# Looks at the weights moved later in the opening, and the first tile of the second deep layer ended a step later, with all-row products of the first keys

## The chip, the cores and the metric

The kernel runs on one core of a Trainium2 chip. Its engines work side by side, each on its own queue of instructions in order, and meet through semaphores: TensorE (PE in the profile, its weight loads PEld), VectorE (DVE), ScalarE (ACT), GpSimd (POOL) and SyncE (SP), which here only issues DMAs. The metric is the device time of one launch in microseconds (us), the median over runs.

## The reference

A transformer layer, fp32, on 8 sequences of 512 rows and 256 features:

```python
x = x + attention(layernorm(x))   # qkv = xn @ qkv_w.T, 16 heads of 16, rotary q and k,
                                  # mask = (same block of 64 | i < 4 | j < 4 | |i - j| <= 128) & (j <= i)
                                  # softmax(q k / 4) @ v, then @ out_w.T
n = layernorm(x)
h = silu((n @ w1.T) * s1) * ((n @ w2.T) * s2)      # 256 -> 1024, weights -1, 0, 1
h = gelu((h @ h1.T) * s1h)                         # 1024 -> 1024, erf form
h = gelu((h @ h2.T) * s2h)                         # 1024 -> 1024
x = x + (h @ w3.T) * s3                            # 1024 -> 256
```

Each query sees at most its own and the previous 128 keys, and the first four keys (the global keys).

## The kernel before, in words

Sequences are worked in rounds. Round r computes the feed-forward layers of sequence r, beside it the attention of sequence a = r + 1, and beside that the normalization, the projections and the rotation (rotary embedding) of sequence b = r + 2. The opening is "round -1": attention of sequence 0 and projections of sequence 1, with no feed-forward. Each engine has a function `beside_attention(r)`, a loop over 20 steps n (16 units of attention, a unit being 4 heads of a tile of 128 queries, and 4 steps of tail). Its body is an order written out by hand; the order of the calls in it is the order on that engine. Rounds 0 to 7 begin with `gated(r)` (w1 and w2), and steps 0 to 15 hold the 16 tiles of the two deep layers on TensorE (tiles 0 to 7 the first, 8 to 15 the second), each in four quarters of two k-chunks (`deep_quarter`), spread between the attention's parts of the step. Bank n % 2 takes tile n. Round 7 has no attention beside it.

Unit n of attention: `scores` (PE, step n), `masked_min` (VectorE: mask, minimum; it frees the bank through `s_free`), `exponentials` (ScalarE), `turn_cur` and `turn_prev` (PE transposes, step n + 2), kept by VectorE (`keep_cur`) and ScalarE (`keep_prev`, n + 2), and `weighted_values` (PE). In the opening the scores of two units come together at even steps, VectorE masks both there, and `values` come at even steps. A tile's last unit adds the products of the four first keys, `Vg` x `PgT` (64 rows: 16 heads x 4 keys), and transposes of `rinv_wide`, then `out_projection` i, VectorE's `residual` i, the second layernorm and its transposes.

All small products share one PSUM bank, MISC (bank 6). `misc_free` reads the order of its users from the lists ROUND and OPENING and waits for the one before to have been read: "o0" is output projection 0, "qk0" to "qk3" the projections of q and k (features 0 and 1), "t" the transposes of the normalized input (kept by ScalarE's `keep_xnT`), "gs", "pg", "vg" the first keys' scores, weights and values, "n" the transposes of the second layernorm.

A hidden tile h is kept as two parts, hi (rounded for the fast product) and lo (the rest). ScalarE makes the full value and hi with `gelu` in parts of 4, 2, 1, 1 tiles, POOL the lo (`deep_lo`), and `deep_split` counts them; tile 8's quarter 3 needs tiles 6 and 7 of layer 0.

The fast product is exact only if the weights have no low bits. ScalarE looks at all weights in 11 looks (`check_weights`, one pass over 128 x 2048 words each, counted in `low_summed`), two before the opening and nine at the steps LOOK_STEPS. At step KNOWN - 1 VectorE takes their maximum (`low_bits`), TensorE turns it into one number, VectorE into a flag (`no_low_bits`), and before step KNOWN TensorE reads it and branches to one of two copies of the rest of its program.

SP's queue in the opening: the loads of inputs; then, after look 3 (`low_summed` 4), the staging of the second layer's weights for the looks; then eight copies of weight chunks from DRAM to DRAM (`w_scratch`, `save_weights`); then `save_split`, which writes the split q and k of sequence 1 to DRAM in four parts, then their loads. ScalarE's `split_hi` 2 and 3 (features 1) write the same SBUF tile that saves 0 and 1 read, so they wait for these saves to have landed:

```python
wait(act, split_saved[1 - f][kind], 16 * SAVES * (b - 1 + f))
```

## Time and profile before

| | |
|---|---|
| time before | 1090.91 us, median of 3 runs (1089.97 to 1091.35) |
| the profiled execution | 1091.03 us, span 1089.2 us |
| mean granted TensorE clock | 0.992 of full speed |
| busy: TensorE, its weight loads, VectorE, ScalarE, POOL | 97%, 81%, 59%, 66%, 41% |
| first gated product | 101.7 us |

The profiled execution's time holds the span, from the first to the last instruction, and some 2 us around it. A profile row of a timeline gives start and length in us, the engine and line, operation and operands, and in brackets how long the engine had stood idle before and what ended that. "issue" means that nothing the profile shows was waited for.

### The profile page before, as it was taken

The numbers are of one execution on the slowest core, as the hardware profiler recorded it, in microseconds if no ns is written. First come the engines' busy times: TensorE is split into PE (matmuls) and PEld (weight loads), VectorE is DVE, ScalarE is ACT, GpSimd is POOL, SyncE is SP. The second block draws the span as 40 slices with busy tenths as digits, with TensorE's granted clock in tenths as the row PEclk, the third lists the DMA queues.
The fourth block names the chain that finished last, engine by engine and source line by source line (L and its number), as shares of the span: only waits on it lengthen the run. The fifth ranks groups of instructions, "written<-read, shape, count | busy, mean of one in ns | idle before, by whom it ended". The sixth has DMA issues, their size and how long they took to land.

```text
span 1089.2 us, 21612 instructions
## 1 busy us (share of the span) xinstructions
PE 1056.3 (97%) x7602; PEld 878.5 (81%) x7602; DVE 643.6 (59%) x1988; ACT 718.4 (66%) x1776; POOL 450.1 (41%) x620
## 2 busy tenths in 40 slices
PE   6788999999999999999999999999999999999998
PEld 3457878898788977889778897889878898789887
DVE  5775576556765567655665566755576555555322
ACT  3895676955958658567586566685676955966422
POOL 5552462433624418235263254442362431532433
PEclk9889999999999999999999999999999999999999
DMA  8887469455655357555483654736556355432540
GB/s 317 306 266 244 162 208 301 131 173 175 197 174 155 125 183 232 144 153 183 134 255 104 194 163 145 241 91 198 170 165 194 108 174 185 115 108 76 178 135 21
DMA packets 112797, 190.16 MB, mean 175 GB/s; under 512 B 7216, under 2 KB 66864, under 8 KB 111664
## 3 DMA queue, kind: packets, MB, share of 16 engines
q1 hardware_dynamic: 112256, 182.45, 53.8%
q10 hardware_dynamic: 432, 6.29, 1.4%
q8 instruction: 64, 1.05, 0.4%
q14 instruction: 45, 0.37, 0.1%
HBM read 150.97 MB, written 45.09 MB: 180 GB/s over the span
## 4 chain that ended last, share of the span: by engine, by line
PE 78%; ACT 10%; DVE 7%; issue 3%; POOL 2%; DMA 1%; SPq 0%; ACTq 0%; DVEq 0%; POOLq 0%
PE bank L787 36%; PE bank L757 11%; PE bank L560 5%; PE bank L691 5%; PE bank L814 4%; PE bank L627 4%; PE bank L657 4%; ACT Sm L963 4%; DVE Sm L1162 3%; PE bank L665 3%; PE bank L591 2%; ACT L983 2%; POOL b_lo L1452 2%; PE bank L716 1%; PE bank L704 1%
## 5 line engine op out<-in xcount | busy, mean ns | idle before, releaser
L963 ACT ACTIVATE Sm<-Sm,smin 128x260 f32<-128x260 f32 (+2 forms) x512 | 241.4, 473 | 163.0 <-DVE smin L1162 162.6
L787 PE MATMUL bank<-b_hi,W 128*128 128x512 f32 x512 | 211.0, 412 | 3.9 <-POOL b_lo L1452 3.9
L787 PE MATMUL bank<-a_hi,W 128*128 128x512 f32 x512 | 206.5, 403 | 0.1
L787 PE MATMUL bank<-b_lo,W 128*128 128x512 f32 x512 | 201.1, 393 | 0.0
L787 PE MATMUL bank<-a_lo,W 128*128 128x512 f32 x512 | 200.8, 392 | 0.0
L757 PE MATMUL bank<-x_hi,W 128*128 128x256 f32 x512 | 125.0, 286 | 0.0
L757 PE MATMUL bank<-x_lo,W 128*128 128x256 f32 x512 | 123.4, 283 | 0.0
L1461 POOL TENSOR_TENSOR a_lo<-a_act,a_hi 128x256 fp32r<-128x256 f32 x128 | 94.4, 741 | 61.7 <-ACT a_hi L1014 61.7
L787 PEld LDWEIGHTS bank<-b_hi,W 128*128 128x128 f32 x512 | 96.4, 188 | 24.8 <-POOL b_lo L1452 10.2
L1162 DVE CUSTOM_DVE_ANT_0 Sm<-bank,msk,gmin 128x256 f32<-128x256 f32 x256 | 108.2, 478 | 10.4 <-PE bank L627 7.0
L1213 DVE TENSOR_SCALAR a_sum<-bank,scales 128x512 f32<-128x512 f32 x64 | 48.0, 750 | 105.7 <-PE bank L787 104.9
L787 PEld LDWEIGHTS bank<-a_hi,W 128*128 128x128 f32 x512 | 96.4, 188 | 17.5 <-DVE a_act L1245 0.3
L787 PEld LDWEIGHTS bank<-a_lo,W 128*128 128x128 f32 x512 | 96.5, 188 | 17.1
L787 PEld LDWEIGHTS bank<-b_lo,W 128*128 128x128 f32 x512 | 96.7, 189 | 14.6
L1452 POOL TENSOR_TENSOR a_lo<-a_act,a_hi 128x512 fp32r<-128x512 f32 x56 | 70.9, 1292 | 83.9 <-ACT a_hi L984 83.9
L757 PEld LDWEIGHTS bank<-x_hi,W 128*128 128x128 f32 x512 | 98.1, 192 | 2.7 <-issue 2.7
L1452 POOL TENSOR_TENSOR b_lo<-b_act,b_hi 128x512 fp32r<-128x512 f32 x64 | 80.9, 1292 | 45.2 <-ACT b_hi L984 45.2
L757 PEld LDWEIGHTS bank<-x_lo,W 128*128 128x128 f32 x512 | 98.1, 192 | 0.0
L1245 DVE SCALAR_TENSOR_TENSOR a_act<-bank,scales,silu 128x256 f32<-128x256 f32 x128 | 61.8, 483 | 58.2 <-ACT silu L1020 57.9
L963 ACT ACTIVATION_READ_ACCUMULATOR Sm<-Sm,smin 128x1 f32 x512 | 96.1, 188 | 0.0
L1213 DVE TENSOR_SCALAR b_sum<-bank,scales 128x512 f32<-128x512 f32 x64 | 47.9, 749 | 76.9 <-PE bank L787 75.9
L1177 DVE COPY PT<-bank 128x512 f32<-128x512 f32 x72 | 49.5, 687 | 70.4 <-PE bank L657 67.7
(134 smaller groups left out, 2199.1 us busy)
## 6 DMA issues: line engine op xcount, KB each, us to landing
W<-w_scratch SPq DMA_DIRECT2D x168, 512.0 KB, 4.1
qk_scratch<-split SPq DMA_DIRECT2D x56, 512.0 KB, 4.0
Qs<-qk_scratch SPq DMA_DIRECT2D x112, 128.0 KB, 4.3
Ks<-qk_scratch SPq DMA_DIRECT2D x14, 1024.0 KB, 8.7
w_scratch<-in_ffn_w SPq DMA_DIRECT2D x22, 512.0 KB, 7.1
x_in<-in_x SPq DMA_DIRECT2D x8, 512.0 KB, 7.5
stage_a<-in_ffn_w ACTq DMA_DIRECT2D x2, 2048.0 KB, 9.6
x<-in_x SPq DMA_DIRECT2D x8, 512.0 KB, 3.9
```

The lines of the kernel that those rows point to most:

```text
L560: mm = nc.tensor.matmul(qk_bank(b, n)[:, :], qkv_w[:, kk, col:col + P], xnT[:, kk, :], start=(kk == 0), stop=(kk == NF - 1))
L627: mm = nc.tensor.matmul(bank[2 + half][:, c2 * KEYS + lo:(c2 + 1) * KEYS], Qs[:, pair, half, :], Ks[:, pair, i * P + lo - P:(i + 1) * P], ...
L691: mm = nc.tensor.matmul(out[32 * c:32 * c + 32, :], v[:, i - 1 + side, col:col + 32], turned(a, n)[:, side, c, :], start=(g == 0 and side ...
L757: mm = nc.tensor.matmul(bank[DOWN_BANKS[s % 4]][:, u * HALF:(u + 1) * HALF], lhsT.bitcast(F32) if general else lhsT, rhs, start=(kk == 0 a ...
L787: mm = nc.tensor.matmul(bank[n % 2][:, :], lhsT.bitcast(F32) if general else lhsT, rhs, start=(kk == 0 and part == 0), stop=(kk == NH - 1 ...
L963: ex = nc.scalar.activation(row, row, ACT.Exp, bias=smin[:, r, c:c + 1], scale=-1.0, accum_out=rowsum[:, i % 2, col:col + 1])
L1162: tt = nc.vector.tensor_tensor_reduce(out=unit_scores(n, lo)[:, c, :], in0=ps[:, c2 * KEYS + lo:(c2 + 1) * KEYS], in1=msk[:, int(i == 1), ...
L1177: nc.vector.tensor_copy(turned(a, n)[:, 1, :, :].rearrange("p c q -> p (c q)"), bank[5][:, :])\
L1213: nc.vector.tensor_scalar((b_sum, a_sum)[layer][:, m, :], bank[n % 2][:, :], scales[:, 2 + layer, m:m + 1], None, ALU.mult).then_inc(sum_k ...
L1245: nc.vector.scalar_tensor_tensor(a_act[:, m, half * HALF:(half + 1) * HALF], bank[DOWN_BANKS[s % 4]][:, HALF:SEQ], scales[:, 1, m:m + 1], ...
L1452: nc.gpsimd.tensor_tensor(lo[:, m, :], full[:, m, :], hi[:, m, :].bitcast(F32), ALU.subtract)\
L1461: nc.gpsimd.tensor_tensor(a_lo[:, m, cols], a_act[:, m, cols], a_hi[:, m, cols].bitcast(F32), ALU.subtract).then_inc(up_split, 1)
```

## The change

Four things change.

1. The looks: LOOK_STEPS becomes (1, 3, 5, 7, 9, 11, 13, 15, 16) from (1, 2, 3, 5, 7, 9, 10, 11, 13), and KNOWN becomes UNITS + 3 = 19 from 16, so the flag is found at step 18 and TensorE branches before step 19. The flag's product goes to bank 2, since the values of sequence 1 are by then in banks 0 and 1.
2. In the opening output projection 0 moves from step 7 to step 10 on TensorE (behind "qk3" in MISC's order), its residual on VectorE and the layernorm scalars on POOL from step 8 to 11. ScalarE's `keep_xnT` comes a step earlier for both halves, the second one behind the exponentials.
3. In every round quarter 3 of tile NH (tile 8) is issued in step NH + 1, behind quarter 0 of tile 9, instead of at the end of step NH.
4. `Vg` and `PgT` get 128 rows, the upper 64 cleared by POOL at the start (`g_zeroed`); the products of the first keys contract over all of them.

```diff
-SHIFT, KNOWN = 3, UNITS
-LOOK_STEPS = (1, 2, 3, 5, 7, 9, 10, 11, 13)
+SHIFT, KNOWN = 3, UNITS + 3
+LOOK_STEPS = (1, 3, 5, 7, 9, 11, 13, 15, 16)
...
-OPENING = ("t0", "t1", "qk0", "qk1", "o0", "qk2", "qk3", "o1", "gs", "pg0", "o2", "n0", "pg1", "n1", "n2", "o3",
+OPENING = ("t0", "t1", "qk0", "qk1", "qk2", "qk3", "o0", "o1", "gs", "pg0", "o2", "n0", "pg1", "n1", "n2", "o3",
...
-        Vg = sb("Vg", [HEADS * NGLOB, EMB])
+        Vg = sb("Vg", [P, EMB])
-        PgT = sb("PgT", [HEADS * NGLOB, P])
+        PgT = sb("PgT", [P, P])
...
                         if t == 0:
-                            pe.wait_ge(low_ready, 1)
+                            pe.wait_ge(s_free, HALVES)
...
                         pe.wait_ge(glob_kept, 2 * a + i - 1)
+                        if a == 0 and i == 2:
+                            pe.wait_ge(g_zeroed, 2)
...
                 if with_f and n < DEEP:
                     deep_quarter(r, n, 0, general)
+                if with_f and n == NH + 1:
+
+                    deep_quarter(r, NH, 3, general)
...
-                if with_f and n < DEEP:
+                if with_f and n < DEEP and n != NH:
                     deep_quarter(r, n, 3, general)
...
-                    if (i := tile_at(n, 7)) is not None:
+                    if r < 0 and n == 10:
+                        out_projection(r, 0)
+                    if (i := tile_at(n, 7)) is not None and (r >= 0 or i):
                         out_projection(r, i)
...
-                    pe.wait_ge(s_free, 2 * (KNOWN - 1))
-                    nc.tensor.matmul(bank[0][0:1, 0:1], low_all[:, :], minus_half, start=True, stop=True)\
+                    pe.wait_ge(s_free, HALVES)
+                    nc.tensor.matmul(bank[2][0:1, 0:1], low_all[:, :], minus_half, start=True, stop=True)\
                         .then_inc(low_added, 1)
                 step(-1, n, False)
+                if n >= UNITS:
+                    v_projection(-1, [n - UNITS])
...
-                    if with_q and nq - 1 in LN1_STEPS:
+                    if r >= 0 and with_q and nq - 1 in LN1_STEPS:
                         keep_xnT(r, nq - 1 - LN1_STEPS[0])
+                    if r == -1 and nq == LN1_STEPS[0]:
+                        keep_xnT(r, 0)
...
                             keep_v(-2, (2, 3))
+                        if r == -1 and nq == LN1_STEPS[1]:
+                            keep_xnT(r, 1)
...
-                        if r < 0 and (i := tile_at(n, 8)) is not None:
+                        if r < 0 and n == 11:
+                            residual(a, 0)
+                        if r < 0 and (i := tile_at(n, 8)) is not None and i:
                             residual(a, i)
...
-                        if n < UNITS + 1 and (i := tile_at(n, 8)) is not None:
+                        if r < 0 and n == 11:
+                            ln2(a, 0)
+                        if n < UNITS + 1 and (i := tile_at(n, 8)) is not None and (r >= 0 or i):
                             ln2(a, i)
...
             pool.wait_ge(q_zeroed, 2)
+            nc.gpsimd.memset(Vg[HEADS * NGLOB:, :], 0.0).then_inc(g_zeroed, 1)
+            pool.wait_ge(g_zeroed, 1)
+            nc.gpsimd.memset(PgT[HEADS * NGLOB:, :], 0.0).then_inc(g_zeroed, 1)
+            pool.wait_ge(g_zeroed, 2)
             pool.wait_ge(consts_loaded, 16)
```

`keep_globals` and `keep_vg` now write rows 0 to 63 by name, and `no_low_bits` reads bank 2.

## Rows read from the trace of the kernel before

**Rows 1.** the page: busy time of each engine, share of the span, instructions

```profile
PE 1056.3 (97%) x7602; PEld 878.5 (81%) x7602; DVE 643.6 (59%) x1988; ACT 718.4 (66%) x1776; POOL 450.1 (41%) x620
```

**Rows 2.** one of the page's costliest groups: busy, mean ns, idle before, releaser

```profile
L787 PEld LDWEIGHTS bank<-b_hi,W 128*128 128x128 f32 x512 | 96.4, 188 | 24.8 <-POOL b_lo L1452 10.2
```

**Rows 3.** table by stretches: length, busy us per engine, clock, DMA share, GB/s

```profile
60.00:80.00 20.00, 15.12 (x151) 9.99 (x154) 16.00 (x54) 19.21 (x53) 10.80 (x20) 0.89 0.74 255
...
80.00:102.00 22.00, 19.25 (x195) 14.33 (x192) 11.83 (x39) 10.94 (x35) 4.01 (x11) 0.94 0.92 290
```

**Rows 4.** timeline of TensorE's weight loads, round 0: start, length, instruction, idle before

```profile
167.71 0.19 PEld L787 LDWEIGHTS bank<-b_lo,W 128*128 128x128 f32 x1
...
168.30 0.19 PEld L787 LDWEIGHTS bank<-b_hi,W 128*128 128x128 f32 x1 [0.40 <-POOL b_lo L1452]
...
169.87 0.66 PEld L627 LDWEIGHTS bank<-Ks,Qs 128*128 128x128 f32 x4
```

**Rows 5.** timeline of POOL and VectorE, round 0

```profile
166.94 2.54 POOL L1452 TENSOR_TENSOR b_lo<-b_act,b_hi 128x512 fp32r<-128x512 f32 x2 [2.61 <-ACT b_hi L984]
...
170.30 0.75 DVE L1213 TENSOR_SCALAR a_sum<-bank,scales 128x512 f32<-128x512 f32 x1
```

**Rows 6.** timeline of the weight loads, round 7

```profile
1052.40 0.19 PEld L787 LDWEIGHTS bank<-b_hi,W 128*128 128x128 f32 x1 [0.64 <-POOL b_lo L1452]
```

**Rows 7.** weight loads grouped by form, and their timeline in round 0

```profile
L700 PEld LDWEIGHTS bank<-PgT,Vg 64*128 64x128 f32 x64 | 8.3, 186 | 3.2 <-issue 3.2
...
203.74 0.52 PEld L700 LDWEIGHTS bank<-PgT,Vg 64*128 64x128 f32 x4 [0.20 <-issue]
...
204.38 0.20 PEld L704 LDWEIGHTS bank<-consts,rinv_wide 128*128 128x128 f32 x2
```

**Rows 8.** timeline of POOL, the first microseconds

```profile
1.76 1.95 POOL L1515 MEMSET Qs<- 64x1024 f32 x2
...
6.21 0.24 POOL L1355 TENSOR_SCALAR ve<-mv 128x2 f32<-128x2 f32 x1 [2.50 <-DVE mv L1091]
```

**Rows 9.** timeline of VectorE, the opening

```profile
51.38 0.72 DVE L1104 STREAM_SHUFFLE rot<-bank 128x512 f32<-128x512 f32 x1
...
54.52 0.48 DVE L1162 CUSTOM_DVE_ANT_0 Sm<-bank,msk,gmin 128x256 f32<-128x256 f32 x1
```

**Rows 10.** timeline of ScalarE, the opening

```profile
31.29 1.91 ACT L1006 ACTIVATE junk<-stage_a 128x2048 uint16<-128x2048 uint16 x1
...
56.26 0.51 ACT L963 ACTIVATE Sm<-Sm,smin 128x260 f32<-128x260 f32 x1 [4.73 <-DVE smin L1162]
...
67.21 0.63 ACT L936 ACTIVATE split<-q 128x512 fp32r<-128x512 f32 x1
...
72.44 0.63 ACT L936 ACTIVATE split<-k 128x512 fp32r<-128x512 f32 x1 [0.27 <-DMA qk_scratch<-split]
...
74.87 0.49 ACT L963 ACTIVATE Sm<-Sm,smin 128x260 f32<-128x260 f32 x1
...
93.29 0.59 ACT L970 COPY PT<-bank 128x512 f32<-128x512 f32 x1 [1.37 <-PE bank L665]
```

**Rows 11.** timeline of SP, which issues the DMAs; landing of the last one's two

```profile
33.32 2.03 SPq L491 DMA_DIRECT2D stage_a<-in_ffn_w  x4
...
36.95 22.26 SPq L411 DMA_DIRECT2D w_scratch<-in_ffn_w  x8
...
61.01 0.90 SPq L381 DMA_DIRECT2D qk_scratch<-split  x2
...
DMA to landing us min/median/max: 4.0/4.6/5.2
```

**Rows 12.** the table by stretches, one of 1 us

```profile
66.00:67.00 1.00, 0.09 (x1) 0.00 (x0) 1.00 (x7) 1.00 (x5) 1.00 (x1) 1.00 0.01 2
```

**Rows 13.** timeline of the weight loads: behind the branch, and step 19

```profile
89.04 0.42 PEld L657 LDWEIGHTS bank<-consts,Sm 128*128 128x128 f32 x4 [1.02 <-ACT Sm L963]
...
98.74 0.73 PEld L716 LDWEIGHTS bank<-out_w,featT 128*128 128x128 f32 x4 [0.46 <-DVE x_lo L1206]
```

More of the change, by code:

```diff
@@ L277, in layer_kernel @@
         q_zeroed = sem("q_zeroed")
+        g_zeroed = sem("g_zeroed")
         q_masked = sem("q_masked")
@@ L976, in keep_globals @@
                 wait(act, pv_done, UNITS * a + (3 * GROUPS if i else 0))
-                nc.scalar.copy(PgT[:, :], MISC[0:HEADS * NGLOB, 0:P]).then_inc(glob_kept, 1)
+                nc.scalar.copy(PgT[0:HEADS * NGLOB, :], MISC[0:HEADS * NGLOB, 0:P]).then_inc(glob_kept, 1)
             def gelu(r, layer, part):
@@ L1142, in keep_vg @@
                 nc.vector.tensor_tensor(
-                    Vg[:, :].rearrange("p (h d) -> p h d", d=HD),
+                    Vg[0:HEADS * NGLOB, :].rearrange("p (h d) -> p h d", d=HD),
                     MISC[0:HEADS * NGLOB, 0:EMB].rearrange("p (h d) -> p h d", d=HD),
@@ L1236, in no_low_bits @@
                 dve.wait_ge(low_added, 1)
-                nc.vector.tensor_scalar(exact_int[:, :], bank[0][0:1, 0:1], 0.0, None, ALU.is_ge).then_inc(low_ready, 1)
+                nc.vector.tensor_scalar(exact_int[:, :], bank[2][0:1, 0:1], 0.0, None, ALU.is_ge).then_inc(low_ready, 1)
             def gated(r):
```

## The prediction

> **What bounds the kernel.** I read the page first. TensorE's matmul row is busy 97% of the span and no other engine more than 66% [rows 1], so from the first gated tile on a gain has to be time in which TensorE stood still, or time that its instructions no longer take. The chain that ended last says the same. Next what TensorE waited for, in the list of waits and in the costliest groups: in the eight rounds it is nearly one thing. The products of a deep tile wait for the low halves `b_lo` that POOL makes, 10.2 us in all before weight loads [rows 2]. The timeline of the weight loads of round 0 shows where: in the last quarter of tile 8, the first tile of the second deep layer. Then the table by stretches for the opening (up to about 102 us). There TensorE is no bound: from 60 to 80 us ScalarE is busy 19.21 of 20 us, from 80 to 102 us only 10.94 of 22 [rows 3]. So in the opening a gain has to be read on ScalarE's timeline, and, as it turns out, on the DMA queue's.
>
> **The last quarter of tile 8, a step later.** In steady work these loads come every 0.23 us. From the load at 167.71 to the scores' first load at 169.87 there are five intervals: 1.16 us at that pace, 2.16 us measured [rows 4]. So 1.00 us is lost in a round. The two operands are POOL's: `b_lo` for kk = 6 and 7, begun at 166.94, finished near 168.2 and 169.48 [rows 5]. In the new order TensorE ends step 8 at 167.94, issues the scores of step 9 (0.59 us), quarter 0 of tile 9 (four loads, 0.93 us), and reaches quarter 3 at 169.46, and the kk = 7 products at 169.93. Both operands are there by then, so the stall goes whole: 7 rounds with attention x 1.00 = 7.0 us. The eighth round has no scores beside it. It waits 0.64 us where 0.04 is usual [rows 6], and quarter 0 of tile 9 alone (0.93 us) covers that: 0.6 us. Sum 7.6 us.
>
> What becomes late in return: tile 8 now ends 169.46 + 0.93 = 170.39 in load times, 0.52 later than 169.87. VectorE's `keep_sum(8)` (at 170.30 before [rows 5]) leads its step 9, and behind it stand the masks of unit 9, `keep_cur(7)`, then ScalarE's exponentials 9 and `keep_prev(7)`; SP's reload of weight slot 0 is 0.5 us later too, and its first reader is eight tiles on. TensorE comes back for `s_free` of unit 9 at 173.94 (one us earlier than before), and the masks end at about 173.2. That leaves 0.7 us. So nothing is charged. The bounds: 7.6 us if all holds, and 3.6 us if half a us is given back in every round at the next wait.
>
> **All-row products of the first keys.** `Vg` x `PgT` used 64 of the array's rows. There are 64 loads of them, four for each of 16 tiles, and the array stood 3.2 us before them, 0.20 each time [rows 7]. Behind them it is the same again: four loads at a pace of 0.11 (the fp32 transposes of 128*128 go at it) are 0.44 us, but from 203.74 the next load comes at 204.38, after 0.64. So each time the array's shape turns costs 0.20 us, and it turns twice. With 128 rows the first turn stays (from the 32-column products), the second goes, because its neighbours behind are 128*128 too. The load should be no dearer: one of 128*128 for a deep tile takes 188 ns [rows 2], one of 64 rows 186 ns [rows 7], so I take over the pace of 0.11. 0.20 us x 14 tiles in the rounds = 2.8 us, and 0.2 us for the one of the opening that lies on its path. From below: 0, if the turn at the end has another reason. The two memsets that clear the idle rows stand on POOL behind the two of 64x1024. POOL waits 2.50 us after these for VectorE's statistics [rows 8]; the new ones have 256 and 128 columns against 2 x 1024 in 1.95 us, so under 0.5 us, hidden. Without that cover they would cost those 0.5 us once.
>
> **The opening.** Four moves act on one chain. (1) Output projection 0 and its residual leave the place between the rotation of keys and the masks of unit 8: there the shuffle ended at 52.10 and the first mask began at 54.52 [rows 9], while ScalarE stood 4.73 us [rows 10]. That is 2.4 us for everything behind it. They land at steps 10 and 11, where the bank has long been free. (2) The normalized input's second half is kept after the exponentials of its step, one step sooner; that takes TensorE's wait for it away, but unit 8 waits for the rotations anyway. (3) One look fewer stands before step 10's `split_hi`: 1.90 us [rows 10]. Together `split_hi(2)` could run at 67.21 - 2.4 - 1.9 = 62.9. (4) Against it stands the queue. SP starts the second layer's staging when look 3 is done, at 33.32. Now exponentials 3 stand before that look: 1.54 us later. Eight copies of weights in DRAM follow, issued till 59.2, and behind them the first save of `split` in two issues, 61.01 and 61.4, of which the later landed near 66.6 (5.2 us) [rows 11]. The DMA engines run near full until about 65 and are down to a share of 0.01 from 66 on [rows 12], so the saves land when the queue has drained, and a queue that starts 1.54 us later drains 1.54 us later: 68.2. `split_hi(2)` must wait for that landing. So it runs not at 62.9 but at 68.2, which is 1.0 later than before.
>
> From there ScalarE needed 7.66 us until exponentials 12 at 74.87. The look of step 10 (1.90) and the wait before the key's split (0.27) are gone: 68.2 + 5.49 = 73.7, that is 1.2 us earlier. Steps 12 to 14 are as they were. The looks of steps 15 and 16 fall where ScalarE idles; it stood 1.37 us before `keep_prev(15)` at 93.29 [rows 10], so the last look sticks out by about 0.5: 0.7 us left, with the all-row product 0.9. Last, the branch. TensorE reads the flag after step 18 now, not 15. Before, the load behind the branch came after 1.02 us idle; at the new place 0.46 us were idle anyway [rows 13]. So 0.56 more, and nothing back at the old place, since there the values wait for ScalarE. Opening: 0.9 - 0.56, some 0.4 us gained.
>
> The Trainium skill has two rules here (Advanced Engine Details and Errata, Control Flow Timing; Runtime: NRT & Kernel Launch, Instruction fetch mechanics). The first puts a compare-and-branch near 0.11 us, by which the opening would gain 0.46 us more and the sum be 1079.7; the second says that a taken branch out of the fetched window waits for a fetch, and the trace's 1.02 us agrees with the second.
> Its page DMA: Bandwidth & Descriptors (Queues, rings and completion order) says that each DMA engine takes descriptors in ring order, and that an increment lands after that engine's earlier writes. The trace agrees as far as the saves landed only when the busy share fell; were the page not to hold, the second rival below would be the likelier.
>
> **The sum.** 7.6 + 2.8 + 0.4 = 10.8 us off the profiled execution's own 1091.03 us (span 1089.2): 1080.2 us. The median, 1090.91, is 0.12 us below that execution, which changes nothing.
>
> **Rivals.** (a) The saves land 5.2 us after their issue as before, whatever stood ahead of them. They are issued at 60.75 at the soonest, `split_hi(2)` runs near 65.7, exponentials 12 at 71.2, 3.7 earlier than before, and the opening gains 3.7 - 0.5 + 0.2 - 0.56 = 2.9: 1077.7 us. For it: no row says whether the issue or the queue set that landing; against it: the share stays full until 65. (b) The opening loses 1 to 2 us, because the queue slips by more than 1.54 us or the branch, now between DRAM copies, costs more: 1081.6 to 1082.6. (c) The second turn of the array stays: 1080.2 + 3.0 = 1083.2. (d) Half of the rounds' gain comes back at the wait for `s_free(9)` or the values' wait for `keep_prev(7)`, both with under 1 us of slack: 1080.2 + 3.6 = 1083.8, or 1087 if all of it does. (e) Slower: tile 8's late sum holds the chain masks, exponentials, turn. It decides when tile 8 ends more than 1.2 us later than before (0.5 + 0.7). To undo 10.8 us and add 2.2 it must cost TensorE 1.7 us a round on top of the 1.0 that the stall cost, so tile 8 some 3.9 us late: about 1093. Nothing between 169.5 and 170.4 could take that long, unless POOL's `b_lo` slipped by as much. (f) No change to be told: the gains are made up elsewhere, 1089 to 1093.
>
> **Chances.** The forecast 0.58, (a) 0.16, (b) 0.10, (c) 0.05, (d) 0.06, (e) 0.03, (f) 0.02. Faster by over 0.2% (2.2 us, about what a measurement of this kernel tells from no change) are all but the last two: 0.95; 0.02 the same; 0.03 slower. The range goes from a us below (a), 1076.5, to (c), 1083.2. What is left out is most of (d), (e), (f) and what is better than (a).
>
> **What would show it.** In every round the weight loads of tile 8's last quarter come at 0.23 us after quarter 0 of tile 9 and no wait for `b_lo` is left; VectorE's sum 8 starts half a us after where it was, and no new wait before the scores of step 10. The loads of `Vg` are 128*128, and those of `rinv_wide` follow without the 0.20 us. In the opening ScalarE stands about 5 us before `split_hi(2)`, named as a DMA's wait, exponentials 8 start some 4.5 us earlier, exponentials 12 about 1.2; the first gated tile starts near 101.3. The prediction is wrong if that ScalarE wait is missing, if a wait for ScalarE or VectorE of over 0.3 us a round appears in steps 10 to 12, or if PgT's products still stand between two gaps.

## The result: 1084.15 us, faster, but by 7 us and not by 11

The changed kernel took 1084.15 us in the median of 5 runs (1083.48 to 1086.4); the kernel before took 1091.35 beside it (5 runs, 1089.97 to 1093.98). The ratio is 0.9935, with an interval of 0.9923 to 0.9947. The direction was right. The size was not: 1080.2 was forecast, and 1084.15 lies above the range's end of 1083.2.

The spans of the two profiled executions are 1089.2 and 1082.3 us, 6.9 apart, so they can be laid side by side. The page of the changed kernel, its busy times and one of its costliest groups, answers to [rows 1, 2]:

```profile
PE 1050.4 (97%) x7602; PEld 878.4 (81%) x7602; DVE 643.6 (59%) x1988; ACT 718.1 (66%) x1776; POOL 450.8 (42%) x622
...
L791 PEld LDWEIGHTS bank<-b_hi,W 128*128 128x128 f32 x512 | 96.5, 188 | 15.1
```

The idle time before the `b_hi` loads fell from 24.8 to 15.1 us and no longer names POOL's `b_lo`. Those 9.7 us are more than the whole kernel gained, so something was paid back. To find where, I cut the span at the first weight load of each round's gated step. These loads come at the same distance in every round to 0.05 us, so a round's length can be compared between kernels, whatever the opening did.

| us | first gated load | rounds 0 to 5, each | round 6 | round 7 to the end | span |
|---|---|---|---|---|---|
| before | 101.67 | 130.66 to 130.70 | 117.86 | 85.64 | 1089.2 |
| changed | 101.11 | 129.90 to 129.93 | 116.56 | 85.12 | 1082.3 |
| gained | 0.56 | 0.76 | 1.30 | 0.52 | 6.9 |

Here is the loss: round 6 gained 1.30 us, rounds 0 to 5 only 0.76. What sets them apart: in rounds 0 to 5 ScalarE also splits the queries and keys of a later sequence beside the deep tiles, in round 6 it has none to split. So less stands in its way there. The weight loads of round 0 in the changed kernel answer to [rows 4]:

```profile
167.38 0.65 PEld L629 LDWEIGHTS bank<-Ks,Qs 128*128 128x128 f32 x4
167.96 0.19 PEld L791 LDWEIGHTS bank<-b_hi,W 128*128 128x128 f32 x1
...
168.78 0.19 PEld L791 LDWEIGHTS bank<-b_hi,W 128*128 128x128 f32 x1
...
169.46 0.19 PEld L791 LDWEIGHTS bank<-b_lo,W 128*128 128x128 f32 x1
169.68 0.59 PEld L659 LDWEIGHTS bank<-consts,Sm 128*128 128x128 f32 x4
...
170.82 0.19 PEld L791 LDWEIGHTS bank<-b_lo,W 128*128 128x128 f32 x1
171.80 0.42 PEld L667 LDWEIGHTS bank<-consts,Sm 128*128 128x128 f32 x4 [0.79 <-ACT PT_a L981]
...
943.55 0.42 PEld L667 LDWEIGHTS bank<-consts,Sm 128*128 128x128 f32 x4 [0.48 <-ACT PT_a L981]
```

The scores, quarter 0 of tile 9 (from 167.96) and then quarter 3 of tile 8 (from 168.78) run at 0.23 us a load; the stall for `b_lo` is gone whole. But two groups further on a new one stands, 0.79 us before `turn_prev(7)`, which turns the scores of unit 7 over the keys of the tile before into bank 4. It waits for ScalarE's `keep_prev(6)`, which copies the turned scores of unit 6 out of that bank. The list of waits gives it as 5.2 us in 7 times, the longest 0.8: six of some 0.78 in rounds 0 to 5, and one of 0.48 in round 6 (the last row above):

```profile
PEld bank L667 <- ACT PT_a L981: 5.2, 7, 0.8
```

ScalarE's timeline in the same place shows what keeps it: the four exponentials of unit 8 stand before the copy.

```profile
167.89 1.28 ACT L974 ACT_TABLE_LOAD   x1
169.18 0.51 ACT L974 ACTIVATE Sm<-Sm,smin 128x260 f32<-128x260 f32 x1
...
171.18 0.56 ACT L981 COPY PT_a<-bank 128x512 f32<-128x512 f32 x1
```

In the kernel before, the copy and the loads of `turn_prev(7)` stood so:

```profile
171.74 0.56 ACT L970 COPY PT_a<-bank 128x512 f32<-128x512 f32 x1
172.65 0.59 PEld L665 LDWEIGHTS bank<-consts,Sm 128*128 128x128 f32 x4
```

The copy ended at 172.30, so there were 0.35 us in hand. Counted from the first gated load, the copy begins at 70.07 us in both kernels (171.74 less 101.67, 171.18 less 101.11), while TensorE was due for the turn at 70.98 and is now due at 69.94, 1.04 sooner. It can go on at 70.69. Of these 0.75 us, 0.18 come back at once, as the four loads of the turn then take 0.38 us to the next and not 0.56: 0.57 us is the price. In round 6 the stall for `b_lo` was longer, 1.22 us beyond the steady pace and not 1.00, and the copy had 0.86 us in hand before; there the new wait of 0.48 us costs 0.27.

The products of the first keys, in round 0 (answers to [rows 7]), and POOL's two new memsets (to [rows 8]):

```profile
202.71 0.52 PEld L704 LDWEIGHTS bank<-PgT,Vg 128*128 128x128 f32 x4 [0.20 <-issue]
203.15 0.25 PEld L708 LDWEIGHTS bank<-consts,rinv_wide 128*128 128x128 f32 x2
203.38 0.47 PEld L659 LDWEIGHTS bank<-consts,Sm 128*128 128x128 f32 x4
```

```profile
3.77 0.31 POOL L1536 MEMSET Vg<- 64x256 f32 x1
4.14 0.20 POOL L1538 MEMSET PgT<- 64x128 f32 x1
```

The four loads now take 0.44 us to the next one, against 0.64: the second turn is gone, the first stays. But the two `rinv_wide` loads behind take 0.23 us to the next, against 0.17 before, so 0.14 is left of 0.20. The memsets lie in POOL's idle 2.50 us.

The opening, as the table by stretches has it (length, then busy us and count of TensorE, its weight loads, VectorE, ScalarE and POOL, the granted clock, DMA share and GB/s; answers to [rows 3]):

```profile
60.00:80.00 20.00, 10.34 (x92) 7.34 (x95) 12.31 (x42) 12.40 (x39) 6.21 (x16) 0.81 0.79 270
80.00:102.00 22.00, 19.87 (x200) 14.99 (x197) 12.04 (x39) 14.42 (x39) 4.55 (x11) 0.94 0.96 297
```

ScalarE fell from 19.21 busy us of 20 to 12.40. Its timeline answers to [rows 10]:

```profile
50.81 0.51 ACT L974 ACTIVATE Sm<-Sm,smin 128x260 f32<-128x260 f32 x1 [1.71 <-DVE smin L1177]
...
69.47 0.63 ACT L947 ACTIVATE split<-q 128x512 fp32r<-128x512 f32 x1 [7.60 <-DMA qk_scratch<-split]
...
74.87 0.50 ACT L974 ACTIVATE Sm<-Sm,smin 128x260 f32<-128x260 f32 x1
...
93.29 0.58 ACT L981 COPY PT<-bank 128x512 f32<-128x512 f32 x1
```

ScalarE ran 5.5 us ahead at unit 8, then stood 7.60 us for one DMA, the save of `split`. At unit 12 (74.87) and at `keep_prev(15)` (93.29) it is where it was before. SP's timeline, which issues that DMA (answers to [rows 11]):

```profile
34.86 1.98 SPq L493 DMA_DIRECT2D stage_a<-in_ffn_w  x4
...
38.54 22.45 SPq L413 DMA_DIRECT2D w_scratch<-in_ffn_w  x8
61.04 10.69 SPq L383 DMA_DIRECT2D qk_scratch<-split  x6
...
61.04 2.46 SPq L383 DMA_DIRECT2D qk_scratch<-split  x1
```

The last line is the first of the six alone: its issue took SP 2.46 us, against 0.38 in the kernel before. The last of the eight copies landed at 66.61 us, against 63.82, and the first save's two transfers by 69.38, against 66.64.

TensorE's weight loads in the opening: the wait that ScalarE's causes, then the way to the first gated step (answers to [rows 13]):

```profile
72.59 0.72 PEld L667 LDWEIGHTS bank<-consts,Sm 128*128 128x128 f32 x4 [6.49 <-ACT PT L981]
...
87.16 0.73 PEld L720 LDWEIGHTS bank<-out_w,featT 128*128 128x128 f32 x4 [0.50 <-issue]
87.92 0.57 PEld L659 LDWEIGHTS bank<-consts,Sm 128*128 128x128 f32 x4
...
90.66 0.73 PEld L593 LDWEIGHTS bank<-qkv_w,xnT 128*128 128x128 f32 x4
...
93.64 0.09 PEld L913 LDWEIGHTS bank<-consts,low_all 128*1 128x1 f32 x2 [0.40 <-DVE low_all L1248]
...
98.18 0.73 PEld L720 LDWEIGHTS bank<-out_w,featT 128*128 128x128 f32 x4 [0.46 <-DVE x_lo L1221]
...
101.11 0.19 PEld L761 LDWEIGHTS bank<-x_hi,W 128*128 128x128 f32 x1 [0.38 <-issue]
```

At the old place of the branch the turn of a unit (87.92) now follows the output projection without the stop of 1.02 us that it had before. At the new place the load behind the branch (98.18) waits 0.46 us for `x_lo`, to the hundredth what it waited before without a branch in front of it.

What the stop of 1.02 us was made of can be read from the rows of TensorE's sequencer in the kernel before (line, operation, count; then shortest, median and longest in ns; first and last start):

```profile
L908 PEldq TENSOR_LOAD <-exact_int x1: 490/490/490, 87.9 to 87.9; - x1
...
L919 PEldq COMPARE_BRANCH  x2: 88/2025/3962, 88.8 to 1083.9; - x2
```

The flag is read into a register (0.49 us, from 87.94), two operations on registers follow, and the branch takes 0.09 and ends at 88.91; the next instruction begins 0.05 us later. So these steps take 0.97 us, half of it the reading, and they fill nearly the whole stop (88.02 to 89.04). In the changed kernel the same steps run from 96.86 to 97.83. Meanwhile loads that had been issued before them go on until 97.73, and `x_lo` is made only by 98.13.

### The profile page after: what moved, and what is told of

Read it like the earlier page. It is cut to its first block, busy times and chain, and to the rows that moved or that the text cites. A ratio compares the mean times of both kernels' runs of the same rounds, so it can differ in the third digit from the quotient of the medians.

```text
span 1082.3 us, 21614 instructions
## 1 busy us (share of the span) xinstructions
PE 1050.4 (97%) x7602; PEld 878.4 (81%) x7602; DVE 643.6 (59%) x1988; ACT 718.1 (66%) x1776; POOL 450.8 (42%) x622
## 4 chain that ended last, share of the span: by engine, by line
PE 79%; ACT 9%; DVE 5%; POOL 3%; issue 2%; DMA 1%; SPq 0%; ACTq 0%; POOLq 0%; DVEq 0%
PE bank L791 35%; PE bank L761 11%; PE bank L818 5%; PE bank L562 5%; PE bank L693 5%; ACT Sm L974 4%; PE bank L629 4%; PE bank L659 3%; PE bank L667 3%; DVE Sm L1177 2%; PE bank L593 2%; ACT L994 2%; PE bank L720 1%; POOL b_lo L1469 1%; PE bank L704 1%
## 5 line engine op out<-in xcount | busy, mean ns | idle before, releaser
L791 PEld LDWEIGHTS bank<-b_hi,W 128*128 128x128 f32 x512 | 96.5, 188 | 15.1
```

Source lines behind the costliest of these rows:

```text
L791: mm = nc.tensor.matmul(bank[n % 2][:, :], lhsT.bitcast(F32) if general else lhsT, rhs, start=(kk == 0 and part == 0), stop=(kk == NH - 1 ...
```

## The experiments

**The parts alone.** Three kernels, each the kernel before with one part of the change: the moved quarter; the all-row products; the opening with looks, flag and moved projection. They ran on one chip with the fourth below; the kernel before took 1092.65 us there (20 runs, 1090.06 to 1095.31).

```diff
 # e1_quarter
+                if with_f and n == NH + 1:
+                    deep_quarter(r, NH, 3, general)
...
-                if with_f and n < DEEP:
+                if with_f and n < DEEP and n != NH:
                     deep_quarter(r, n, 3, general)
```

> The kernel before with one part of the change alone: tile 8's last quarter a step later. Theory A (the stall of 1.00 us is gone, but the transposes turn_prev(7), now reached 1.0 us sooner, wait for ScalarE's keep_prev(6), which frees their bank; about 0.37 us a round is left in rounds 0 to 5, 1.1 in round 6, 0.5 in round 7): span shorter by about 3.7 us, a new wait of some 0.8 us before turn_prev in six rounds. Rival B (the prediction's term, 1.00 us a round, is right for this part alone, and what is missing was lost by its meeting the other parts): shorter by 7.6 us and no such wait.

Measured: 1089.08 us (5 runs), ratio 0.9961 (0.9945 to 0.9977). Rounds 0 to 5 take 130.20 to 130.22 us, 0.47 less than before; round 6 takes 116.83, 1.03 less; round 7 takes 85.12, 0.52 less. In all 4.4 us from the first gated load on; the profiled execution as a whole doesn't show it, since its first gated load came only at 106.21. The new wait is there with nothing else changed:

```profile
176.90 0.42 PEld L665 LDWEIGHTS bank<-consts,Sm 128*128 128x128 f32 x4 [0.78 <-ACT PT_a L972]
```

So the quarter itself brings the new wait. It is 0.78 us in rounds 0 to 5 and 0.49 in round 6, where more had been in hand and 1.03 us of the gain are left. The expectation had the wait in six rounds only; it stands in seven.

```diff
 # e2_rows
-        Vg = sb("Vg", [HEADS * NGLOB, EMB])
-        PgT = sb("PgT", [HEADS * NGLOB, P])
+        Vg = sb("Vg", [P, EMB])
+        PgT = sb("PgT", [P, P])
```

(with the two memsets, their semaphore, and the copies named by rows, as in the change)

> The kernel before with the all-row products alone (128 rows of Vg and PgT, the upper half cleared). Theory A: 0.20 us at each of 14 tiles in the rounds, since the turn of the array's shape behind the products goes: span shorter by 2.8 to 3.0 us, each round by 0.40. Rival B (the loads of 128 rows take as much longer as the turn cost, or POOL's memsets reach the first layernorm): within 0.3 us of before.

Measured: 1089.75 us (10 runs), 0.9973 (0.9963 to 0.9983). Rounds 0 to 5 take 130.41 to 130.44, round 6 takes 117.61: 0.25 less in each, for two tiles. So 0.125 us a tile, 1.75 us for the 14 tiles.

```diff
 # e3_opening: the change without these
-                if with_f and n == NH + 1:
-                    deep_quarter(r, NH, 3, general)
...
-        Vg = sb("Vg", [P, EMB])
-        PgT = sb("PgT", [P, P])
+        Vg = sb("Vg", [HEADS * NGLOB, EMB])
+        PgT = sb("PgT", [HEADS * NGLOB, P])
```

> The opening's part alone (looks, flag, output projection 0, keep_xnT), rounds and products as before. Theory A: ScalarE gains about 5 us up to step 10, loses them all in one wait of about 7.6 us for the first save of split, and the first gated product comes 0.2 to 0.4 us sooner; span shorter by 0.2 to 0.4. Rival B (the opening was worth more and the all-row products cost it something): shorter by over 1 us. The branch: if it costs 0.56 us more at its new place, no gain at all.

Measured: 1092.1 us (10 runs), 0.9996 (0.9982 to 1.0009). Its first gated load comes at 101.73 (101.67 before), and rounds have the lengths of before. The opening's whole rebuild is worth nothing that can be told. Where ScalarE's lead went, its timeline shows:

```profile
69.78 0.63 ACT L942 ACTIVATE split<-q 128x512 fp32r<-128x512 f32 x1 [7.59 <-DMA qk_scratch<-split]
```

**The unit kept first.** The changed kernel, with `keep_prev(6)` moved ahead of the exponentials of unit 8 on ScalarE, in the rounds:

```diff
 # e4_keep_first
+                        if r >= 0 and n == NH:
+                            keep_prev(a, n - T_LAG)
                         if n < UNITS:
                             exponentials(a, n)
...
-                        if GROUPS <= n - T_LAG < UNITS:
+                        if GROUPS <= n - T_LAG < UNITS and (r < 0 or n != NH):
                             keep_prev(a, n - T_LAG)
```

> The changed kernel, and ScalarE copies keep_prev(6) ahead of exponentials 8 in every round, not behind them. Theory A (turn_prev(7) waits for this copy alone): the copy ends near 169.8 instead of 171.7 in round 0, the wait of 0.79 us is gone, rounds 0 to 5 are shorter by 0.6 us each, span about 1078.6. Rival B (exponentials 8 come 0.56 us later, and TensorE waits for them or for what follows from them): less than 1 us gained, or a loss.

Measured: 1080.91 us (4 runs), 0.9895 (0.9878 to 0.9912). Rounds 0 to 5 take 129.35 to 129.37, another 0.57 less, and round 6 takes 116.29, another 0.27 less: in each the price that was read above. The copy now comes before the table load, and the turn that waited for it follows at once (ScalarE's timeline, then the weight loads'):

```profile
167.97 0.57 ACT L981 COPY PT_a<-bank 128x512 f32<-128x512 f32 x1
168.56 1.28 ACT L974 ACT_TABLE_LOAD   x1
```

```profile
171.03 0.19 PEld L791 LDWEIGHTS bank<-b_lo,W 128*128 128x128 f32 x1
171.26 0.59 PEld L667 LDWEIGHTS bank<-consts,Sm 128*128 128x128 f32 x4
```

With 0.47 from the quarter alone that makes 1.04 us a round, close to the 1.00 that the prediction had read for the stall for `b_lo`.

**The control.** A gain by a reordering could be the reordering's own. So the same edit went into the kernel before, without the change.

> The kernel before, with the keeping of the sixth tile's turned scores ahead of the eighth tile's exponentials in the rounds, and nothing of the change. It is the control of the run in which this edit took another 0.57 us a round off the changed kernel (129.93 to 129.36). Theory A: the edit is worth time only because the moved quarter brought TensorE to the turn of the seventh tile before the bank was kept; without the move TensorE arrives 0.3 us after it, so rounds stay at 130.66 to 130.70 and the time at 1090 to 1092 (or up to 0.1 us a round worse, as the exponentials of the eighth tile come 0.56 later). Rival E: ScalarE's order in this place costs the kernel before the same 0.57 us a round, and the gain had nothing to do with the quarter: rounds of 130.1, time 4 us down to 1087.

Measured: 1092.86 us (10 runs) against 1092.79 (15 runs), 1.0006 (0.9995 to 1.0018). Rounds 0 to 5 take 130.66 to 130.70 as before, and both stalls for `b_lo` are where they were:

```profile
169.56 0.19 PEld L787 LDWEIGHTS bank<-b_hi,W 128*128 128x128 f32 x1 [0.40 <-POOL b_lo L1454]
...
170.80 0.19 PEld L787 LDWEIGHTS bank<-b_hi,W 128*128 128x128 f32 x1 [0.93 <-POOL b_lo L1454]
```

So ScalarE's order is worth 0.57 us a round only behind the moved quarter. It was no bound before.

**The wait covered from TensorE's side.** In the changed kernel quarter 2 of tile 9 goes ahead of `turn_prev(7)`:

```diff
 # e5_quarter2_first
+                if with_f and n == NH + 1:
+                    deep_quarter(r, n, 2, general)
                 if with_a and 0 <= t < UNITS and not (values and with_f):
                     turn_prev(a, t)
-                if with_f and n < DEEP and not values:
+                if with_f and n < DEEP and not values and n != NH + 1:
                     deep_quarter(r, n, 2, general)
```

> The changed kernel with the third quarter of the ninth tile's deep products (eight products with their weight loads) ahead of the turn of the seventh tile, so that TensorE has some 1.9 us of other work in the place where it waits 0.79 us for ScalarE. Theory A: the wait goes as it did when ScalarE kept the tile sooner, so a round takes 129.36 to 129.5 and the time is 1080.5 to 1082. Rival F: that quarter has a wait of its own (its split weights, or a bank that is free later), or the values' products and the kept halves behind it come later by the 1.9 us and hold somebody up: a round of 129.9 or more, 1084 or slower.

Measured: 1082.0 us (4 runs), 0.9903 (0.9884 to 0.9921), rounds of 129.37 to 129.38, the same as with the copy moved. The turn has no wait left:

```profile
173.16 0.59 PEld L667 LDWEIGHTS bank<-consts,Sm 128*128 128x128 f32 x4
```

The quarter is four loads, 0.93 us of work and not the 1.9 that was expected, and that was enough: the copy ends at 172.91, 0.25 us before the turn. Two cures that have only this wait in common give the same round to 0.02 us (round 6: 116.29 and 116.30). The cause of the rounds' shortfall is settled by that.

**The queue ahead of the saves.** The changed kernel, with four instead of eight weight copies on SP's queue ahead of the saves of `split`:

```diff
 # e6_early4
-EARLY = 8
+EARLY = 4
```

> The changed kernel with four instead of eight weight copies queued ahead of the saves of q0 and k0 (EARLY 8 to 4), all else the same. Theory A: in the changed opening ScalarE is ready for the second unit's split at 61.9 us and stands 7.6 us for the saved q0 and k0, which can't be issued before the eight copies of 22.45 us each from issue to landing have room in the queue (saves issued at 61.0). With four copies ahead the saves are issued some 10 us sooner, the wait of 7.6 falls below 2, the first gated step starts between 95 and 99 instead of 101.1, and the time is 1078 to 1081 us (4 to 6 below the changed kernel); round lengths stay 129.93. Rival B: the saves are late because q0 and k0 themselves are staged late, not because of the queue: the wait stays over 6 us and the time stays 1083 to 1085. Rival C: the copies now issued later delay the loads of the saves by the same time, or the looks further down become the bound: the wait goes, but 60 per cent or more of it comes back before the first gated step (100 to 101).

Measured: 1079.78 us (4 runs), 0.9885 (0.9862 to 0.9908); the changed kernel had 0.9935. First gated load at 96.28, 4.83 sooner; rounds unchanged at 129.93. SP's timeline, and ScalarE's:

```profile
39.12 15.13 SPq L413 DMA_DIRECT2D w_scratch<-in_ffn_w  x4
55.88 10.71 SPq L383 DMA_DIRECT2D qk_scratch<-split  x6
```

```profile
62.37 0.63 ACT L947 ACTIVATE split<-q 128x512 fp32r<-128x512 f32 x1 [0.17 <-DMA qk_scratch<-split]
...
67.50 0.63 ACT L947 ACTIVATE split<-k 128x512 fp32r<-128x512 f32 x1 [2.06 <-DMA qk_scratch<-split]
```

The saves go out 5.16 us sooner and `split_hi(2)` runs 7.10 us sooner. The kernel before, with the same edit:

> The kernel before with the same single edit (EARLY 8 to 4). Theory A: in the opening of before ScalarE is busy with looks until 67.2 and waits only 0.27 us for the saves, so sooner saves bring 0 to 0.5 us on the profiled opening (first gated step at 101.2 to 101.7), but executions whose saves landed later (first gated step at 104.2 and 106.2 seen with this same opening) come back to it: median 1089.5 to 1091, a narrower spread of its single times than 1090.1 to 1095.3. Rival C: the later copies cost the opening 1 us or more: 1092 to 1094.

Measured: 1091.45 us (10 runs) against 1091.73, 0.9991 (0.9978 to 1.0003). No change, and that part of the expectation held: there the saves were issued at 61.74, with a queue half as long, because q0 itself is split only at 59.46 and VectorE has its low half ready at 61.72. In the kernel before, the copies had been issued by 59.2 and q0's low half was ready at 60.98, with the save issued at 61.01. The change made the low half ready at 55.53, and the queue then held the save until 61.04. The other part fell: the single times spread from 1088.96 to 1095.83, no narrower than before. This profiled execution had its first gated load at 106.46, and ScalarE waited 2.05 us before it could split k, where the profiled kernel before waited 0.27. In the table by stretches (here TensorE alone: busy us and count, clock, DMA share, GB/s) it had the lower of TensorE's two clocks, 1.2 GHz, throughout 70 to 75 us, and that of the kernel before for about half of the time. In the 5 us ahead of it TensorE had been busy 2.77 us in this one and 2.75 in the other.

```profile
70.00:75.00 5.00, 4.59 (x58) 0.76 1.01 350
```

```profile
65.00:70.00 5.00, 2.77 (x35) 0.89 0.12 45
70.00:75.00 5.00, 5.00 (x27) 0.50 1.01 371
```

(the first from the kernel before, the other two from this one)

**One look back at step 2**, so that its staging buffer is free sooner:

```diff
 # e8_look3, on the changed kernel
-LOOK_STEPS = (1, 3, 5, 7, 9, 11, 13, 15, 16)
+LOOK_STEPS = (1, 2, 5, 7, 9, 11, 13, 15, 16)
```

> The changed kernel with the second look back at step 2 (looks at 1, 2, 5, 7, 9, 11, 13, 15, 16 instead of 1, 3, 5, ...), all else the same. Theory A: the look frees its staging buffer for the next weights, whose copies stand ahead of the saves on SP's queue, so with this look sooner the queue drains 1 to 2 us sooner: saves issued at 59 to 60, the wait at the second unit's split falls from 7.6 us to 3.5 to 5 (1.9 of it because ScalarE arrives later with the look ahead), TensorE's start of the gated step at 99.5 to 100.5, time 1082.5 to 1083.5. Rival D: the landing is set by something the look doesn't touch (ring room of all 16 queues, or the staging of q0 and k0): the split stays at 69.5 and the time at 1084 to 1085, the look being hidden in the wait.

Measured: 1084.56 us (4 runs, 1082.76 to 1085.03), 0.9929 (0.9906 to 0.9951). In the profile the direction is as said: SP's copies start at 38.40, the saves go out at 60.17, and the wait shrinks, though not to the 3.5 to 5 us that were expected:

```profile
67.92 0.63 ACT L947 ACTIVATE split<-q 128x512 fp32r<-128x512 f32 x1 [5.46 <-DMA qk_scratch<-split]
```

The first gated load comes at 99.63, 1.48 sooner. But the median doesn't show it; the expected 1082.5 to 1083.5 was missed. Inconclusive: one execution profiled, and a median of four that can't tell 1.5 us.

**Both cures together**, with four copies ahead of the saves and then with two:

> The changed kernel with both edits: the keeping of the sixth tile's turned scores ahead of the eighth tile's exponentials in the rounds (which alone gave 1080.9 us and rounds of 129.36), and four copies ahead of the saves. The two lie in different stages, so they add: Theory A 1074.5 to 1077, rounds of 129.36 and a first gated step at 95 to 99. Rival B or C of the opening: 1080 to 1081.

> The changed kernel with the sixth tile kept first, and two weight copies ahead of the saves instead of four. With four ScalarE still waited 2.1 to 2.3 us at the split of the second unit's k, and about 0 at q. Theory A: what is left of the wait is the distance of the saves from each other and of the sixth save from its load, which two copies fewer bring forward by up to 5 us less what ScalarE needs itself: wait at k below 1 us, first gated step 0.5 to 2 us sooner than with four (96.5 to 94.5), 1075 to 1077 us. Rival C: the saves can't be issued before their staging in either case (q0 and k0 are split at 55 and later), so the copies ahead are no longer what is waited for: no change, 1076 to 1078. Rival G: the copies issued later than the saves delay the weights that the looks read: first gated step later than 97, over 1078.

Measured: 1077.03 us (5 runs, 1076.16 to 1080.69), 0.9870 (0.9848 to 0.9893), and 1075.70 us (5 runs, 1075.48 to 1076.6), 0.9846 (0.9832 to 0.9860). Rounds take 129.35 to 129.37 in both; the first gated load comes at 96.54 and 97.26. The first median is 0.03 us above the upper end of what was expected from adding the two. Of two copies against four nothing can be said: the intervals overlap, the profiled opening was even 0.7 later (past the 97 us that rival G had named, though not with its 1078 us), and the wait at k was 2.26 us where 2.32 was. The first condition of each, rounds of 129.36, held. The wait at k below 1 us did not come. The trace with two copies says what sets it, and it isn't the queue: the save of k0 also needs the low half of k0, which VectorE makes behind the masks of its step though the high half had been ready since 56.97:

```profile
61.49 0.96 DVE L1131 SCALAR_TENSOR_TENSOR split<-k,split 128x512 fp32r<-128x512 f32 x1
```

That ends at 62.45, the save is issued at 62.48, lands at 67.12, and ScalarE splits k at 67.21. With four copies it is the same way from 61.98 to 66.84. Moving that low half ahead of the masks would be the next thing to try; no run here did. Both medians lie below those of the kernels with one cure (1080.91 and 1079.78), and 1.3 to 1.5% below the kernel before.

## Why the prediction was wrong

**Where it failed.** The step that failed is "So nothing is charged" behind the moved quarter, and with it the term 7.6 us. It checked the wait for `s_free` of unit 9 and the values' wait for `keep_prev(7)`, which lie behind. It did not check a wait nearer by, that of `turn_prev(7)` in the same step 9 as the moved products, for which ScalarE must have finished `keep_prev(6)`. That had 0.35 us in hand before, and TensorE came a full us sooner. The wait gave back 0.57 us in each of the rounds 0 to 5 and 0.27 in round 6, 3.7 us in all; shown by the quarter alone (4.4 us, not 7.6), by the two cures, and by the control. Nor would the sign of being wrong have pointed there, as it named steps 10 to 12. The fourth rival had the kind and the size right (half of the rounds' gain back, 1083.8 us) and the place wrong, and it had 0.06. The last round gave 0.52, not 0.6. Without the wait the quarter would have given more than forecast, not less: the stall was worth 1.04 in rounds 0 to 5 and 1.30 in round 6, where 1.00 was taken for each.

**Right in mechanism, off in size.** The term 2.8 us for the all-row products measured 1.75. The gap behind goes, as said, but its neighbours run slower by 0.06 us, so a turn saved is worth 0.125 and not 0.20. The third rival (no gain) is out.

**The opening: 0.4 forecast, 0.56 measured, by other steps.** `split_hi(2)` was to run at 68.2 and ran at 69.47: the first save landed 2.74 us later than in the profiled kernel before (69.38, 66.64) and not 1.54, and the last copy 2.79 later. The save's issue was itself held up, 2.46 us where it took 0.38 before. That ate all of the 1.2 us expected at unit 12. But the profiled kernel before was itself a lucky execution in this: in three others with its order of the opening (quarter alone, all-row products alone, the control) the first save landed at 70.10, 70.03 and 68.61, and ScalarE stood 3.17, 2.72 and 1.95 us for it before `split_hi(2)`. So how much of the slip is the change's can't be told, and ScalarE was not always the only bound of that opening, as the prediction had read from one execution.

On the other side the branch was charged 0.56 us and cost nothing, since the same wait for `x_lo` of 0.46 us covers it; nor does the 1.02 us agree with the rule of a fetch, as the prediction says, for the branch itself took 0.09 us with the next instruction 0.05 behind it. Nor was it right that nothing comes back at the old place: with the 1.02 us stop gone, the value projection behind it is loaded at 90.66 and not at 91.24, 0.58 sooner. The flag's product takes 0.14 of that, the all-row product adds 0.13, and so the 0.56 comes out, though ScalarE begins its `keep_prev(15)` at 93.29 in both. In the kernel with the opening alone, where `split_hi(2)` ran another 0.31 us later, the first gated load came 0.06 us the wrong way, so the opening's part is not to be told from zero.

The first rival (saves landing 5.2 us after their issue at 60.75, and ScalarE's split near 65.7, where its own terms give 65.95) is out: the issues began at 61.04, the second only at 63.54, and the save had landed 8.4 us after the first began. That the queue ahead of the saves sets it, which the prediction argued from the DMA share, is now shown by the run with four copies. The Trainium skill's rule in DMA: Bandwidth & Descriptors (Queues, rings and completion order), that each engine takes its descriptors in ring order, fits this run: `split_hi(2)` ran 7.10 us sooner with four copies fewer ahead of the save.

**Summed up**, from the first to the last instruction: opening 0.56, quarter 4.39, all-row products 1.79, and 0.20 that the two do together beyond what each does alone: 6.9 us. Forecast were 0.4, 7.6 and 2.8.

## What to carry to other kernels

When a stall on the bounding engine is removed, everything behind it on that engine comes sooner by its length. Check the very next wait of each kind first, and write down for each how long its producer had been done: whatever had less in hand than the stall removed is the next stall, and the gain is little more than what it had in hand (here 0.35 us in hand and 0.47 gained of 1.04, in round 6 0.86 in hand and 1.03 gained of 1.30). Then look for the cheap second step: here one copy moved ahead of four exponentials gave the missing half back.

When an engine is relieved in a stage that it bounds, look for what else ends there at the same time. ScalarE and the queue of copies came together within a few us, so a rebuild of ScalarE's opening alone gave nothing that can be told, and a constant changed from 8 to 4, worth nothing that can be told before, gave 5 us after it. And look at a second execution of such a stage before taking its waits for granted.

## What the runs showed of the hardware

- A gated round repeats from round to round, and from execution to execution, to 0.05 us, while the opening of the kernel before, in one and the same order, had its first gated load at 101.67, 102.94, 104.21 and 106.21 us in four executions (the third with the all-row products in it). The later ones also waited longer for the first save before `split_hi(2)`: 0, 1.95, 2.72 and 3.17 us. The granted clock of TensorE goes with it too: 0.92 and 0.74 in 75 to 80 and 80 to 85 us in the first of these, 0.50 in both in the kernel with the quarter alone, which had 106.21. In the 5 us ahead TensorE had been busy 4.59 us in the first and 1.21 in the other. Why one execution gets the lower clock there and another doesn't stays open; the spread of whole times is the opening's, which is why round lengths, and not medians, separated most of these runs.
- Between loads of 64x128 and of 128x128 the weight loading stood 0.20 us, with nothing waited for. Making both 128x128 took the gap away but gave 0.125 us: the two loads that follow take 0.23 us to the next and not 0.17.
- To branch on a flag that another engine computed took 0.97 us from the start of its reading to the end of the branch: 0.49 us to read it (0.48 to 0.49 in every run here), 0.09 for the branch. It cost nothing to be seen where loads issued before it and a wait for data lay over it. The Trainium skill (Runtime: NRT & Kernel Launch, Instruction fetch mechanics) says that a taken branch out of the fetched window waits for a fetch. At this branch the trace shows none, the next instruction being 0.05 us behind. The second branch of the same line, at 1083.9 us, where the last products of the program still ran, took 3.96 us; what it waited for the trace doesn't show.
